# An AdaLN block with attention and a two-of-eight expert layer: merged attention loads, filler products in every free step, earlier first loads, later gates, and a shorter router pipeline

## The chip, the cores and the metric

The kernel runs on one NeuronCore of a Trainium2 chip. It is one program with one launch. TensorE (PE) multiplies, VectorE (DVE) and ScalarE (ACT) work element by element, GpSimd (POOL) does the rest, and SyncE (SP) issues most transfers between the chip's memory (DRAM, for short) and the on-chip memory. The metric is the device time of one execution in microseconds, and lower is better. Of three runs of the kernel before, the median is 2024.34 us (2022.81 to 2042.44).

## The reference, cut to what matters

x is (2, 2048, 256), float32 throughout. H = 16 heads of 16, 6 lattice and 6 hex codes, 8 experts with 1024 hidden units.

```
mod = (silu(c) @ wmod).reshape(2, 6, 1, 256)            # sa, ca, ga, sb, cb, gb
ga, gb = (2*(g >= 0) - 1) * max(|g|, 0.25)               # the two gates
h = layernorm(x) * (1 + ca) + sa
q, k, v = split(h @ qkv_w.T)                             # 16 heads of 16
scores = alpha * tanh(q k^T / beta)
       + sigmoid(lam)/2 * tanh(h hex^T) tanh(h hex^T)^T  # one for all heads
       + lattice(head, tanh(h q6^T), tanh(h q6^T))       # per head
x = x + ga * (softmax(causal(scores)) v) @ out_w.T
h = layernorm(x) * (1 + cb) + sb
logits = silu(h @ rw1 + rb1) @ rw2 + rb2                 # 4096 tokens, 8 experts
top 2, softmax of the two
out = x + gb * sum over the two experts of p_e * (silu(h @ w1[e] + b1[e]) @ w2[e] + b2[e])
```

## The kernel before, in words

The program runs stages one after another. `stage_modulation` loads x (4 MB in four parts) and wmod, gets the statistics of every row of x on VectorE, and the six modulation rows of both batches on TensorE; VectorE evacuates them into `modrow` and finishes the gates there (four operations behind a copy for each of the four gate rows, each waited for). `stage_front` holds the projections and the attention. `stage_output` multiplies by out_w, applies ga and adds x. `stage_router` computes logits, chooses two experts for each token and scatters the token's row to its places in `x_rows`. `stage_experts` takes 72 tiles of 128 rows through their expert. Each stage is a block that all engines enter together.

**The attention.** Eight blocks of 512 queries (two batches of four), each with four groups of four heads: 32 iterations. An iteration has a step for every 128 keys that the block sees, three of them on the diagonal, in all 288 steps. A step is: raw scores of four heads (`raw_scores`, TensorE), tanh of 2048 columns (ScalarE), the bilinear part of each head (`bilinear`, TensorE), a sum for each head (`score_sum`, VectorE), exp (ScalarE), a mask on the diagonal (POOL) and the weighted values (`weighted_values`, TensorE). TensorE is three steps ahead with raw scores, there are four buffers of probabilities.

float32 products are made of halves. A raw score contracts 64 rows: q's high and low halves against k's halves (hi, lo, lo, hi). In memory `q_split` and `k_split` keep two halves a head; a load puts them into the 64 rows in several pieces. A bias row set has 50 rows: 24 of the lattice (`lat_split`), 24 of the hex codes (`soft_split`, one for all heads, spread by the load) and two of a guard (`guard_split`).

**Projections.** The parts of a block's projections are T0, T1 (transposes of h), C (codes), Q0 to Q3 (q and k), L (lattice), V0, V1 and G (guard). Blocks 0 and 1 are projected before attention starts (`HEAD_PARTS`), in five banks; the parts of the others are spread over attention steps by `SLOT`, half a part a step. A step without one may have a filler, `keep_clock`: a product whose result nobody reads. `FILL_AT` gives it to a step that is two or more (three or more behind C) behind the last projection. POOL splits codes, lattice, guard and later Q parts into halves (`split_codes`, `split_lattice`, `split_guard`, `split_heads`), and masks, all in one queue. Before it overwrites a half it waits for the stores of the last block's.

**SP's queue in `stage_front`.** It is in order: x of blocks 0 and 1 and the projection weights; the stores of block 0; `load_keys(0)`; V; codes; guard; `load_bias(0)`, `load_values(0)`; x of block 2; the loads of iteration 1; the stores of block 1; and then, step by step, stores as parts are done, loads of iteration it when iteration it-2 is nearly done (`KEYS_AT`, `BIAS_AT`, `VALUES_AT`), and the stores of the output. `load_keys` waits for the stores of all four Q parts of its block and issues ten loads, `load_bias` waits for three kinds of stores and issues six.

**The router.** It is a pipeline over eight blocks of 512 tokens, written by `skewed` with a lag of five: in step m, VectorE places block m-5 and chooses for block m-4, evacuates the logits of block m-3, splits h of block m-1 and normalises block m. TensorE transposes the logits of m-4, ranks m-5, multiplies logits of m-3, transposes m-1 and multiplies the hidden units of m-2 (eight chunks in three banks). ScalarE takes the tanh of the logit difference of m-5 and then eight silus of m-2. POOL scatters eight tiles of a block once it is placed.

Of the kernel before, what the change touches and what calls it, by code (L numbers as in the profile page):

```python
# [146 lines left out]
def build(nc, a, out):  # L147
# [16 lines left out]
    with ExitStack() as ctx:  # L164
# [5 lines left out]
        with ExitStack() as c2:  # L170
# [3 lines left out]
            stage_modulation(nc, a, modrow, ident, scal, shift, rstd, lattice)  # L174
            stage_front(nc, a, dram, modrow, ident, scal, shift, rstd, lattice, rows_sb, x_back)
# [39 lines left out]
def stage_modulation(nc, a, modrow, ident, scal, shift, rstd, lattice):  # L215
    with ExitStack() as ctx:
# [9 lines left out]
        gate = sb("gate", [P, D])  # L226
        gate_abs = sb("gate_abs", [P, D])
        gate_sign = sb("gate_sign", [P, D])
# [21 lines left out]
        def _(sp):  # L250
# [8 lines left out]
            for q in range(1, XQ):  # L259
                load_x(sp, q)  # L260

        @block.scalar
        def _(act):
# [9 lines left out]
            act.activation(rstd[:, :], rstd[:, :], ACT.Sqrt).then_inc(std_ready, 1)  # L273

# [13 lines left out]
        def _(dve):  # L288
# [59 lines left out]
            for b in range(B):  # L348
                for part in range(6):
                    cols = slice((b * 6 + part) * D, (b * 6 + part + 1) * D)  # L350
                    if part % 3 == 0:
                        dve.tensor_copy(modrow[:, cols], mod_ps[:, cols])
                    elif part % 3 == 1:
                        dve.tensor_scalar(modrow[:, cols], mod_ps[:, cols], 1.0, None, ALU.add)
                    else:
                        then_wait(dve.tensor_copy(gate[:, :], mod_ps[:, cols]))
                        then_wait(dve.scalar_tensor_tensor(gate_abs[:, :], gate[:, :], -1.0, gate[:, :],
                                                           ALU.mult, ALU.max))
                        then_wait(dve.tensor_scalar(gate_abs[:, :], gate_abs[:, :], 0.25, None, ALU.max))
                        then_wait(dve.tensor_scalar(gate_sign[:, :], mod_ps[:, cols], 0.0, 2.0,  # L360
                                                    ALU.is_ge, ALU.mult))
# [4 lines left out]
def stage_front(nc, a, dram, modrow, ident, scal, shift, rstd, lattice, rows_sb, x_back):  # L366
    with ExitStack() as ctx:
# [14 lines left out]
        def borrow(n):  # L382
            used[0] += n
            return rows_sb[:, used[0] - n:used[0]]
# [1359 lines left out]
```

## Time and profile before

| | |
|---|---|
| median of three runs | 2024.34 us |
| the profiled execution | 2022.98 us |
| its span | 2021.2 us |
| busy: PE, PEld, DVE, ACT, POOL | 1811.4, 1076.5, 1209.0, 1233.8, 512.2 us |
| mean granted TensorE clock | 0.926 |
| DMA | 280.29 MB in 186101 packets, mean 139 GB/s |
| first product of attention (raw scores, L800) | 102.1 us |
| last filler product (L788) | 1230.1 us |
| filler products | 222 instructions in 111 steps |
| hidden products of the router (L1314) | 1322.4 to 1436.9 us |

The span in 40 equal slices of 50.5 us:

```profile
PE   2868999999999979999999997689559999999997
ACT  1157889989989968999999993234213333333332
POOL 0535331331232333411000001405612222222222
PEclk7768879989989979999999998889779999999999
```

Each digit is a busy share in tenths; PEclk is the TensorE clock that was granted, in tenths of 2.4 GHz. The attention fills the slices from the third to the twenty-fifth, the experts those from the thirtieth on. A filler is two instructions, since a float32 product takes two passes.

### The profile page before, as it was taken

The numbers are of one execution on the slowest core, as the hardware profiler recorded it, in microseconds if no ns is written. First come the engines' busy times: TensorE is split into PE (matmuls) and PEld (weight loads), VectorE is DVE, ScalarE is ACT, GpSimd is POOL, SyncE is SP. The second block draws the span as 40 slices with busy tenths as digits, with TensorE's granted clock in tenths as the row PEclk, the third lists the DMA queues.
The fourth block names the chain that finished last, engine by engine and source line by source line (L and its number), as shares of the span: only waits on it lengthen the run. The fifth ranks groups of instructions, "written<-read, shape, count | busy, mean of one in ns | idle before, by whom it ended". The sixth has DMA issues, their size and how long they took to land. (4 is left out here: it accounts for less than half of the span.)

```text
span 2021.2 us, 33603 instructions
## 1 busy us (share of the span) xinstructions
PE 1811.4 (90%) x10688; PEld 1076.5 (53%) x10689; DVE 1209.0 (60%) x2539; ACT 1233.8 (61%) x1292; POOL 512.2 (25%) x535
## 2 busy tenths in 40 slices
PE   2868999999999979999999997689559999999997
PEld 1333333333334333333333334568459999999997
DVE  7446768878778757778777775867313333333332
ACT  1157889989989968999999993234213333333332
POOL 0535331331232333411000001405612222222222
PEclk7768879989989979999999998889779999999999
DMA  4489674564562477754844404631366666666663
GB/s 152 122 215 187 157 149 102 118 121 110 121 126 70 114 186 147 138 124 108 191 76 76 87 6 133 203 122 69 110 204 182 182 180 175 186 181 181 176 183 79
DMA packets 186101, 280.29 MB, mean 139 GB/s; under 512 B 18512, under 2 KB 120784, under 8 KB 183824
## 3 DMA queue, kind: packets, MB, share of 16 engines
q1 hardware_dynamic: 172272, 259.94, 51.1%
q0 software_dynamic: 13440, 17.97, 4.5%
q8 instruction: 58, 0.95, 0.2%
q10 hardware_dynamic: 288, 1.08, 0.2%
q14 instruction: 43, 0.35, 0.1%
HBM read 213.90 MB, written 65.03 MB: 138 GB/s over the span
## 5 line engine op out<-in xcount | busy, mean ns | idle before, releaser
L963 DVE SCALAR_TENSOR_TENSOR probs<-probs,scal,bil_ps 128x512 f32<-128x512 f32 (+1 forms) x1152 | 788.2, 715 | 286.2 <-PE bil_ps L817 233.5
L896 ACT ACTIVATE probs<-probs 128x2048 f32<-128x2048 f32 (+1 forms) x288 | 522.7, 1815 | 101.5 <-DVE probs L963 101.0
L889 ACT ACTIVATE probs<-raw_ps 128x2048 f32<-128x2048 f32 (+1 forms) x288 | 508.9, 1767 | 28.9 <-PE raw_ps L800 28.4
L817 PE MATMUL bil_ps<-u_mv,w_st 50*128 50x512 f32 (+3 forms) x1280 | 470.9, 469 | 38.0 <-DVE probs L963 33.5
L817 PEld LDWEIGHTS bil_ps<-u_mv,w_st 50*128 50x128 f32 x1280 | 196.3, 192 | 528.9 <-DVE probs L963 448.6
L1635 ACT ACTIVATE hid_t<-fc_ps,b 128x128 f32<-128x128 f32 x576 | 156.3, 382 | 403.4 <-PE fc_ps L1602 236.0
L836 PE MATMUL o_ps<-probs,v_sb 128*32 128x512 f32 (+3 forms) x2560 | 314.5, 575 | 19.4 <-POOL probs L714 13.2
L800 PE MATMUL raw_ps<-q_mv,k_st 64*128 64x512 f32 (+3 forms) x1280 | 270.8, 406 | 15.2 <-DMA q_mv<-q_split 9.5
L1602 PE MATMUL fc_ps<-rows_t,w 128*128 128x128 f32 x2304 | 270.5, 276 | 0.0
L1602 PEld LDWEIGHTS fc_ps<-rows_t,w 128*128 128x128 f32 x2304 | 264.6, 193 | 0.1
L1613 PE MATMUL fc_ps<-w,hid_t 128*128 x1152 | 260.5, 379 | 0.0
L714 POOL TENSOR_SCALAR_AFFINE_SELECT probs<-probs 128x512 f32<-128x512 f32 x128 | 79.5, 634 | 615.6 <-ACT probs L896 614.2
L1613 PEld LDWEIGHTS fc_ps<-w,hid_t 128*128 128x128 f32 x1152 | 213.4, 190 | 26.3 <-issue 0.2
L1576 POOL DMA_INDIRECT out<-y,token x72 | 112.1, 1557 | 432.7 <-DVE y L1687 423.0
L1683 DVE TENSOR_TENSOR y<-fc_ps,b 128x256 f32<-128x256 f32 x72 | 30.6, 424 | 300.3 <-PE fc_ps L1613 300.3
L800 PEld LDWEIGHTS raw_ps<-q_mv,k_st 64*128 64x128 f32 x1280 | 145.1, 196 | 28.3 <-ACT probs L889 9.8
L788 PE MATMUL part_ps<-modrow,ident 128*128 128x512 f32 x222 | 127.5, 657 | 0.0
L836 PEld LDWEIGHTS o_ps<-probs,v_sb 128*32 128x32 f32 x2560 | 54.2, 111 | 96.6 <-issue 78.2
L1361 POOL DMA_INDIRECT x_rows<-rows_sb,place x64 | 62.6, 978 | 103.3 <-DVE place L1390 85.9
L1343 ACT ACTIVATE act_t<-hid_ps,rb 128x512 f32<-128x512 f32 x64 | 44.0, 689 | 61.2 <-PE hid_ps L1314 61.2
L1679 DVE SCALAR_TENSOR_TENSOR gate<-modrow,late 128x256 f32<-128x256 f32 x72 | 35.0, 485 | 46.8 <-DVE share L1672 46.1
L760 PE MATMUL part_ps<-rows_sb 128*128 128x512 f32 x100 | 61.4, 700 | 0.0
(213 smaller groups left out, 1356.9 us busy)
## 6 DMA issues: line engine op xcount, KB each, us to landing
w<-in_w SPq DMA_DIRECT2D x80, 1024.0 KB, 6.0
q_mv<-q_split SPq DMA_DIRECT2D x128, 128.0 KB, 7.6
k_st<-k_split SPq DMA_DIRECT2D x48, 256.0 KB, 8.5
rows<-x_rows SPq DMA_DIRECT2D x72, 130.0 KB, 2.2
v_rows<-rows_sb SPq DMA_DIRECT2D x8, 1024.0 KB, 7.7
o_t<-o_sb SPq DMA_DIRECT2D x32, 256.0 KB, 9.4
k_st<-k_split SPq DMA_DIRECT2D x16, 512.0 KB, 8.6
v_sb<-v_rows SPq DMA_DIRECT2D x8, 1024.0 KB, 13.6
```

What stands on the lines that cost most here:

```text
L714: ins = pool.affine_select(out=tri, in_=tri, compare_op=ALU.is_ge, fill=0.0, base=0, pattern=[[0, HG], [1, P]], channel_multiplier=-1)
L788: pe.matmul(part_ps[:, :], ident[:, :], modrow[:, 0:BLK], start=True, stop=True)
L800: mm = pe.matmul(raw_ps[:, hd, column:column + width], k_st[row:row + ROWS, p, hd // 2, kt * P:(kt + 1) * P], q_mv[row:row + ROWS, p, hd / ...
L817: mm = pe.matmul(bil_ps[:, hd % 2, column:column + width], w_st[row:row + BIAS_ROWS, b, kt * P:(kt + 1) * P], u_mv[row:row + BIAS_ROWS, p, ...
L836: mm = pe.matmul(o_ps[hd * VW:(hd + 1) * VW, query:query + width], v_sb[:, p, kt, hd * VW:(hd + 1) * VW], probs[:, s % NBUF, hd, column:co ...
L889: act.activation(probs[:, s % NBUF, :, first:BLK], raw_ps[:, :, first:BLK], ACT.Tanh).then_inc(tanh_ready, 1)
L896: act.activation(scores, scores, ACT.Exp).then_inc(exp_ready, 1)
L963: dve.scalar_tensor_tensor(scores, scores, scal[:, ALPHA:ALPHA + 1], bil_ps[:, hd % 2, first:BLK], ALU.mult, ALU.add).then_inc(sum_ready, 1)
L1576: pool.indirect_dma_start(out, bass.IndirectOffsetOnAxis(ap=token[:, u:u + 1], axis=0), y[:, u % 2, :], None, compute_op=ALU.add).then_inc ...
L1602: mm = pe.matmul(fc1_ps[:, p, hc * P:(hc + 1) * P], w1[:, q, k, hc * P:(hc + 1) * P], rows_t[:, p, k * P:(k + 1) * P], start=(k == 0), sto ...
L1613: mm = pe.matmul(fc2_ps[:, p, 0:D], hid_t[:, p, hc * P:(hc + 1) * P], w2[:, ds(e * (HC * D) + hc * D, D)], start=(hc == 0), stop=(hc == HC ...
L1635: silu = act.activation(hid_t[:, p, cols], fc1_ps[:, p, cols], ACT.Silu, bias=b1[:, ds(e * HC + hc, 1)])
```

## The change

It does seven things.

1. `q_split` and `k_split` keep four halves a head, in the order in which the rows are contracted, so each Q part is stored in four pieces. Keys are loaded by one transfer and queries by one.
2. Lattice, codes and guard are stored into one tensor, `u_split`, of 50 rows a head; the six soft rows are stored once for each of 16 heads, by a source that repeats. A bias load is two transfers.
3. Block 0's Q2 and Q3 are stored by ScalarE's queue, its other parts in the order Q0, Q1, C, L by SP's.
4. Every step without a projection gets a filler. Behind C it is one of 64 output rows, beside the codes' 12, and doesn't wait.
5. The first loads of x and the projection weights are issued in the modulation stage, behind its own.
6. The gates are only copied in the modulation, two of four groups of columns by ScalarE. The output stage finishes all four gate rows at once, before its first tile.
7. The router's lag is three: block m-3 is chosen, ranked and placed in the step in which its logits are multiplied; TensorE ranks it between the fourth and the fifth hidden chunk.

```
@@ schedule
-        if half != 0 and s >= last + (3 if o == "C" else 2):
-            FILL_AT[s] = (i, o)
+        assert half != 0
+        FILL_AT[s] = (i, o)
@@ scratch tensors
-    scratch("q_split", (B * H * 2 * HD, T))
-    scratch("k_split", (B * H * 2 * HD, T))
-    scratch("lat_split", (B * H * 4 * HEX, T))
-    scratch("soft_split", (B * 4 * HEX, T))
+    scratch("q_split", (B * H * 4 * HD, T))
+    scratch("k_split", (B * H * 4 * HD, T))
+    scratch("u_split", (B * H * BIAS_ROWS, T))
-    scratch("guard_split", (B * H * 2, T))
@@ stage_modulation, SP, behind its own loads
+            for i in range(EARLY):
+                row = BLOCKS[i][0] * T + BLOCKS[i][1] * BLK
+                sp.dma_start(x_blk[:, i, :, :], a["x"][row:row + BLK, :].rearrange("(t p) d -> p t d", p=P)
+                             ).then_inc(xb_in[i], 16)
+                if i == 0:
+                    sp.dma_start(wcode[:, :, :], a["code_wt"].rearrange("(k p) n -> p k n", p=P)).then_inc(p_in, 16)
+                    sp.dma_start(wqkv[:, :, :], a["qkv_wt"].rearrange("(k p) n -> p k n", p=P)).then_inc(p_in, 16)
...
@@ stage_modulation, ScalarE
+            act.wait_ge(mod_done, 1)
+            for b in range(B):
+                cols = slice((b * 6 + 2) * D, (b * 6 + 4) * D)
+                act.activation(modrow[:, cols], mod_ps[:, cols], ACT.Copy)
@@ stage_modulation, VectorE
-                    if part % 3 == 0:
+                    if part % 3 == 1:
+                        dve.tensor_scalar(modrow[:, cols], mod_ps[:, cols], 1.0, None, ALU.add)
+                    elif part in (0, 5):
                         dve.tensor_copy(modrow[:, cols], mod_ps[:, cols])
-                    else:
-                        then_wait(dve.tensor_copy(gate[:, :], mod_ps[:, cols]))
...
@@ stage_front
+        def store_heads(eng, i, m):
+            b, c = BLOCKS[i]
+            halves = (qk_hi, qk_lo, qk_hi, qk_lo) if m < 2 else (qk_hi, qk_lo, qk_lo, qk_hi)
+            for part, src in enumerate(halves):
+                eng.dma_start(part_rows("q_split" if m < 2 else "k_split", H, 4, HD,
+                                        slice((m % 2) * 8, (m % 2) * 8 + 8), part, b, c),
+                              src[:, m, :].bitcast(F32)).then_inc(st_qk[m], 16)
@@ store of C
-                        sp.dma_start(part_rows("soft_split", 1, 4, HEX, slice(0, 1), part, b, c),
-                                     (s_hi, s_lo)[part % 2][HEX:HROWS, :].bitcast(F32)).then_inc(st_s, 16)
+                        src = (s_hi, s_lo)[part % 2][HEX:HROWS, :].bitcast(F32).rearrange("r (o t) -> r o t", o=1)
+                        sp.dma_start(bias_rows(i, (4 + part) * HEX, HEX).rearrange("z h r t -> r (z h) t"),
+                                     src.broadcast_to([HEX, H, BLK])).then_inc(st_s, 16)
@@ load_keys
-                for z in range(2):
-                    row = z * ROWS
-                    load(k_st[row:row + 2 * HD, p, :, seen], k_both[z])
...
+                for dst, name, cols in ((k_st[:, p, :, seen], "k_split", seen), (q_mv[:, p, :, :], "q_split", own)):
+                    rows = heads(name, ROWS, i, g, cols).rearrange("(j r) t -> r j t", r=2 * ROWS)
+                    sp.dma_start(dst.bitcast(F32), rows).then_inc(keys_in[p], 16)
@@ load_bias
-                    load(u_mv[row:row + n, p, :, :], lat[z])
-                    load(u_mv[row + n:row + 2 * n, p, :, :], sf.broadcast_to([n, HG // 2, BLK]))
-                    load(u_mv[row + 2 * n:row + BIAS_ROWS, p, :, :], gd[z])
+                    sp.dma_start(u_mv[z * ROWS:z * ROWS + BIAS_ROWS, p, :, :].bitcast(F32), rows[z]
+                                 ).then_inc(bias_in[p], 16)
@@ SP, head of the stage
-            for o in ("Q0", "C", "Q1", "Q2", "L", "Q3"):
+            for o in ("Q0", "Q1", "C", "L"):
                 store(0, o)
@@ keep_clock
                 if o == "C":
-                    pe.wait_ge(code_ready, i + 1)
+                    pe.matmul(part_ps[ROWS:P, :], ident[:, ROWS:P], modrow[:, 0:BLK], start=True, stop=True)
@@ ScalarE, block 0
+                if i == 0:
+                    for m in (2, 3):
+                        act.wait_ge(emptied, EMPTIED[i, f"Q{m}"])
+                        store_heads(act, i, m)
@@ stage_output, VectorE
+            gates = modrow[:, :].rearrange("p (g s d) -> p g s d", s=3, d=D)[:, :, 2, :]
+            dve.scalar_tensor_tensor(gate_abs[:, :, :], gates, -1.0, gates, ALU.mult, ALU.max).then_inc(gate_step, 1)
+            dve.tensor_scalar(gate_sign[:, :, :], gates, 0.0, 2.0, ALU.is_ge, ALU.mult)
+            dve.wait_ge(gate_step, 1)
+            dve.tensor_scalar(gate_abs[:, :, :], gate_abs[:, :, :], 0.25, None, ALU.max).then_inc(gate_step, 1)
+            dve.wait_ge(gate_step, 2)
+            dve.scalar_tensor_tensor(gates, gate_sign[:, :, :], -1.0, gate_abs[:, :, :], ALU.add, ALU.mult
+                                     ).then_inc(gate_step, 1)
@@ stage_router, TensorE: order within a step
-                if active(4): transpose of the logits      (first in the step)
-                if active(5): rank
                 if active(3): logit products
                 if active(1): transposes of h
+                if active(3): transpose of the logits
-                if active(2): hidden, chunks 0 to 7
+                if active(2): hidden(m - 2, u % 2, range(HC // 2))
+                if active(3): rank
+                if active(2): hidden(m - 2, u % 2, range(HC // 2, HC))
@@ stage_router, ScalarE, ahead of the silus
-                if active(5):
-                    act.wait_ge(logit_diff_ready, m - 5 + 1)
+                if active(3):
+                    act.wait_ge(logit_diff_ready, m - 3 + 1)
@@ stage_router, VectorE: order within a step
-                if active(5): place_rows(m - 5)
-                if active(4): choose(m - 4)
                 if active(3): copy of the logits
                 if active(1): the two splits of h
+                if active(3): choose(m - 3); place_rows(m - 3)
                 if active(0): normalise(m, u)
```

The router's lines are shortened here to their order; what each does has not changed.

## Rows read from the trace of the kernel before

**Rows 1.** Stages: span, busy us of PE, PEld, DVE, ACT, POOL; PEclk, DMA share, GB/s.

```profile
102.00:190.00 88.00, 67.18 (x338) 28.59 (x339) 46.62 (x75) 52.41 (x33) 40.07 (x48) 0.71 0.92 208
...
700.00:760.00 60.00, 47.20 (x258) 19.91 (x258) 35.88 (x57) 40.02 (x25) 25.69 (x28) 0.80 0.75 178
...
1000.00:1210.00 210.00, 209.43 (x1103) 79.17 (x1103) 162.40 (x236) 202.71 (x117) 9.96 (x16) 1.00 0.36 65
```

**Rows 2.** Eight stretches of low clock, columns as in group 1: first and sum.

```profile
230.00:245.00 15.00, 13.47 (x58) 4.98 (x56) 11.00 (x17) 11.01 (x7) 3.37 (x3) 0.66 0.90 254
...
sum 105.00, PE 97.21 PEld 33.70 DVE 61.70 ACT 76.51 POOL 45.13; mean PE 12.15 PEld 4.21 DVE 7.71 ACT 9.56 POOL 5.64
```

**Rows 3.** Timeline of two full steps, start us, us, engine: tanh, filler, tanh.

```profile
1204.05 1.87 ACT L889 ACTIVATE probs<-raw_ps 128x2048 f32<-128x2048 f32 x1
...
1205.03 1.13 PE L788 MATMUL part_ps<-modrow,ident 128*128 128x512 f32 x2
...
1211.30 1.86 ACT L889 ACTIVATE probs<-raw_ps 128x2048 f32<-128x2048 f32 x1
```

**Rows 4.** Timeline of the modulation, first and last evacuation, and of the first normalisation.

```profile
27.68 0.42 DVE L352 COPY modrow<-mod_ps 128x256 f32<-128x256 f32 x1
...
38.52 0.42 DVE L362 SCALAR_TENSOR_TENSOR modrow<-gate_sign,gate_abs 128x256 f32<-128x256 f32 x1
...
43.35 0.41 DVE L472 TENSOR_SCALAR rows_sb<-rows_sb,rstd,shift 128x256 f32<-128x256 f32 x1 [4.40 <-DMA rows_sb<-in_x]
```

**Rows 5.** Timeline of VectorE at the start of the output stage.

```profile
1234.22 0.28 DVE L1151 MEMSET blank<- 128x260 f32 x1 [3.41 <-PEq L367]
...
1239.81 0.26 DVE L1163 RECIPROCAL rden<-o_tr_ps 128x16 f32<-128x16 f32 x1 [2.77 <-PE o_tr_ps L1099]
```

**Rows 6.** DMA, 10 to 24 us, in 40 slices: busy tenths and GB/s, x and wmod.

```profile
DMA  9999999999999999999999999999994000000000
GB/s 404 456 386 404 345 342 360 357 351 345 360 342 345 354 348 348 345 354 348 351 337 351 351 351 348 339 360 342 360 275 135 23 0 0 0 0 0 0 0 0
```

**Rows 7.** DMA, 130 to 140 us, keys, queries and bias, in 40 slices.

```profile
DMA  9998999999999999999899998778999899987998
...
DMA packets 1235, 1.85 MB, mean 185 GB/s; under 512 B 253, under 2 KB 428, under 8 KB 1233
```

**Rows 8.** DMA, 64 to 68 us, the two stores of Q0, in 40 slices.

```profile
DMA  0000576292420913344743564448353554455445
GB/s 0 0 0 0 143 123 61 20 82 20 41 20 0 102 20 82 123 164 164 246 164 143 205 266 184 164 164 287 123 184 143 225 225 184 164 225 225 184 164 205
```

**Rows 9.** Timeline of POOL and of PE, the first iterations.

```profile
89.70 0.60 POOL L664 CAST w_hi<-code 12x512 fp32r<-12x512 f32 x1
...
114.67 1.81 POOL L714 TENSOR_SCALAR_AFFINE_SELECT probs<-probs 128x512 f32<-128x512 f32 x3
...
139.81 1.22 PE L800 MATMUL raw_ps<-q_mv,k_st 64*128 64x512 f32 x4 [9.48 <-DMA q_mv<-q_split]
```

**Rows 10.** Timeline of one router step.

```profile
1382.93 0.71 PE L1314 MATMUL hid_ps<-h_hi,rw_hi 128*128 128x512 f32 x2
...
1384.67 0.69 ACT L1343 ACTIVATE act_t<-hid_ps,rb 128x512 f32<-128x512 f32 x1 [3.48 <-PE hid_ps L1314]
...
1384.94 1.21 DVE L1452 CAST h_hi<-tr_ps 128x1024 fp32r<-128x1024 f32 x1
```

**Rows 11.** Timeline of the end of the router.

```profile
1438.06 1.96 PE L1293 MATMUL log_ps<-act_t,rw 128*32 128x128 f32 x64 [0.30 <-ACT act_t L1343]
...
1444.75 0.18 DVE L1394 TENSOR_TENSOR logits<-lgt_ps,rb 128x32 f32<-128x32 f32 x1
...
1446.28 0.17 DVE L1406 TENSOR_TENSOR logit_diff<-top 128x4 f32<-128x4 f32 x1
...
1450.35 0.16 DVE L1390 CAST place<-place_f 128x8 uint32<-128x8 f32 x1
...
1469.28 0.96 POOL L1361 DMA_INDIRECT x_rows<-rows_sb,place  x1 [0.31 <-issue]
```

More of the change, by code:

```diff
@@ L415, in stage_front @@
         part_ps = ps("part_ps", [P, BLK])
-        p_in, pad_ready, ones_ready = sem("p_in"), sem("pad_ready"), sem("ones_ready")
-        x_in = [sem(f"xb_in{p}") for p in range(2)]
+        pad_ready, ones_ready = sem("pad_ready"), sem("ones_ready")
         h_ready, part_mm, emptied, code_ready, hi_ready = (
@@ L489, in load_rows, with bias_rows @@
                              ).then_inc(x_in[i % 2], 16)
+            def bias_rows(i, first, n):
+                view = dram["u_split"].rearrange("(z h r) t -> z h r t", h=H, r=BIAS_ROWS)
+                b, c = BLOCKS[i]
+                return view[b:b + 1, :, first:first + n, c * BLK:(c + 1) * BLK]
             def store(i, o):
@@ L507, in store @@
                         sp.wait_ge(lo_ready, 4 * (i - EARLY) + m + 1)
-                    for part, src in enumerate((qk_hi, qk_lo)):
-                        sp.dma_start(part_rows("q_split" if m < 2 else "k_split", H, 2, HD,
-                                               slice((m % 2) * 8, (m % 2) * 8 + 8), part, b, c),
-                                     src[:, m, :].bitcast(F32)).then_inc(st_qk[m], 16)
+                    store_heads(sp, i, m)
                 elif o == "L":
@@ L1305, in step, with hidden @@
                     tr.then_inc(tr_mm, 1)
+                if active(3):
+                    pe.wait_ge(log_ready, m - 3 + (LOG_0 + 1))
+                    pe.transpose(lgt_ps[:, 0:P], log_sb[:, :], ident[:, :]).then_inc(lgt_mm, 1)
                 if active(2):
[L1307 to L1316 removed]
+                    hidden(m - 2, u % 2, range(HC // 2))
+                if active(3):
+                    n = m - 3
+                    pe.wait_ge(rank_step, n * N_RANK + N_RANK)
+                    flat = lambda t: t.rearrange("p t e -> p (t e)")
+                    pe.matmul(rank_ps[:, 0:TPB * E], before[:, :], flat(both[:, :, :]), start=True, stop=False)
+                    pe.matmul(rank_ps[:, 0:TPB * E], all_ones[:, :], flat(seen[:, 0:TPB, :]),
+                              start=False, stop=True).then_inc(rank_mm, 1)
+                if active(2):
+                    hidden(m - 2, u % 2, range(HC // 2, HC))
+            def hidden(n, p, chunks):
+                if chunks[0] == 0:
+                    pe.wait_ge(h2_t_step, n * 2 + (H2T_0 + 2))
+                for hc in chunks:
+                    pe.wait_ge(act_ready, n * HC + (bank_before(hc) + 1 + ACT_0))
+                    terms = [(w, x, k) for w, x in ((rw1_hi, h2_hi), (rw1_hi, h2_lo), (rw1_lo, h2_hi))
+                             for k in range(KC)]
+                    for j, (w, x, k) in enumerate(terms):
+                        mm = pe.matmul(hid_ps[:, hc % HB, :], w[:, k * HID + hc * P:k * HID + (hc + 1) * P],
+                                       x[:, p, k, :], start=(j == 0), stop=(j == len(terms) - 1))
+                    mm.then_inc(hid_mm, 1)
             pe.sem_inc(log_mm, LOGM_0)
@@ L1320, in _ @@
             pe.sem_inc(hid_mm, HIDM_0)
-            skewed(pe, N_RBLK, 5, 2, step)
+            skewed(pe, N_RBLK, 3, 2, step)
             pe.wait_ge(place_ready, N_RBLK + PL_0)
@@ L1465, in _ @@
             dve.wait_ge(seen_ready, 1)
-            skewed(dve, N_RBLK, 5, 2, step)
+            skewed(dve, N_RBLK, 3, 2, step)
             done = [0]
```

124 lines of the change are left out of this document (45 added, 79 removed).

## The prediction

> **What bounds the kernel now.** I read the busy strips of the page first, then a table by stage, then the waits, the DMA view and timelines of the places that the diff touches. Four stretches matter. From 102 to 190 us, the first attention steps, ScalarE is busy 52.4 of 88 us, the DMA engines 92%, and the clock is 0.71 [rows 1]. From 1000 to 1210 us attention runs at its pace: ScalarE 202.7 of 210 us (0.965), TensorE as full, clock 1.00. So a steady step is ScalarE's tanh and exp, 3.62 us ((1211.30 - 1204.05)/2), and a filler product fits into it [rows 3]. Between 190 and 1000 us ScalarE loses time where the clock falls: in eight stretches, 105 us together, it is busy 76.5 us [rows 2], where 0.965 would give 101.3; 24.8 us are lost. In the one at 230 us the step behind a finished G part has neither a projection nor a filler, TensorE idles there, and some ten microseconds at the lower level (1.2 GHz) follow. Last, the experts' stage is TensorE's own chain, and nothing in the change touches it.
>
> **The change, part by part.** The sum is against the profiled execution: 2022.98 us (span 2021.2), 1.4 below the median of 2024.34.
>
> **1. Modulation.** VectorE evacuates and finishes the gates from 27.68 to 38.94 us, and normalises block 0 from 43.35 us, behind loads of x that are issued at its stage's start [rows 4]. Of 24 operations 8 stay, at about 0.34 us each ((38.52 - 27.68)/32 for the mean of 32, short waits in it; so 2.7 us). ScalarE's two copies of 512 columns run beside them. The stage ends near 30.4 us, plus 0.5 for the handover: 30.9. The loads moved forward are 1.8 MB behind the 5.8 MB of x and wmod; those moved at about 350 GB/s with the engines at 9 tenths and were over at about 21 us [rows 6], so the rest takes 5.2 us more, and lands before 30.9. Issuing costs SP's time alone, and SP has nothing else there. Saved: 43.35 - 30.9 = 12.4 us. The row's wait of 4.40 us, less the handover, is for the load of x: if the loads came late, those 3.9 would be paid again, and the term would end at -8.5.
>
> The gates' four operations on 1024 columns come back in the output stage. VectorE is free from 1234.50 and next needed at 1239.81 [rows 5]; an operation on 1024 columns takes 1.21 us [rows 10], so at most 4.9 with short waits. Hidden by the wait for the first transposed tile, 0; without that cover 4.9.
>
> **2. Merged loads, doubled stores, 102 to 190 us.** Keys, queries and bias now go to 16 or 32 partitions at a time. With them in the queue the engines are 9 tenths busy and move 185 GB/s [rows 7]; x into 128 partitions moves 350 at the same share [rows 6]. The merged loads cover 128 partitions (bias 50). A first-block iteration loads 1.4 MB: 7.6 us become 4.0; a second-block one 1.9 MB: 10.3 become 5.4. The schedule asks for iterations 2 to 6 in the stretch, of which about half are second-block ones: some 18 us of DMA time less. SP issues 5 loads an iteration instead of 17, which costs nothing and frees it.
> Against it: each Q part is stored in four pieces instead of two. The stores of Q0 ran at some 180 GB/s with only 4 to 5 tenths busy [rows 8], as if half the engines carried them. Eight more of 256 KB a block at 185 GB/s: 11 us a block on that half. New too is soft, stored 16 times over: 4 x 192 KB a block, all read from six partitions. Nothing in the trace reads like it. Bounds: at the rate of rows 8, 1.0 us each, 4 a block; at the narrow loads' rate scaled by partitions (185 x 6/32 = 35 GB/s) 5.5 each, 22 a block. I take the 22, since a few partitions are what it is nearest to.
> The Trainium skill, "SBUF — State Buffer", section "Door 1: The DMA port swizzle", says that what counts is how many of 16 ports the partitions reach, 27.2 GB/s each; by it the six partitions reach two, and the four on one take about 4.8 us a store, 19 a block. The trace agrees on the loads (185 GB/s on 32 partitions or fewer); no row here shows the store.
> Who waits: POOL splits block 1's codes at 89.70 without a gap, and its mask at 114.67 [rows 9] starts the first weighted values. The change makes that split wait for block 0's soft stores: issued by about 74, beside 11 us of Q, with 22 of their own, they land near 98 or 99, 9 us later (an estimate: Q0's pieces start at 63, twelve pieces of 0.7 us of issue lie ahead, and a wait for Q1). The eight pieces of Q2 and Q3 of block 0 are issued by ScalarE, some 5 us of its queue; nothing of its own is due there until block 1's codes, and its high half of Q3 for block 1 comes after the same 98 us, so 0. Then block 1's stores sit in the queue ahead of the keys of iteration 2, for which TensorE already waits 9.48 us until 139.81 [rows 9]. So the first 40 us get up to 9 longer, and what follows gets back about as much. I take 0; ends -18 (the loads' gain whole, the stores beside it) and +20 (stores 11 + 22 on top of each other for block 1, less 13 won back in the iterations behind).
> The second batch starts at 700 us the same way: 40.0 busy of 60 [rows 1], 17.9 below pace. Part is masks behind POOL's code split, which stays; I take -5, ends -10 and +3.
>
> **3. Fillers.** 62 more steps get one, all those that had neither (173 of 288 steps are without a projection, 111 had a filler). In each stretch of rows 2 such a step stands just ahead. A filler is two products of 0.43 us apart, 1.13 us with its drain [rows 3], beside ScalarE: 0 at full clock. I take three quarters of the 24.8: -18; ends -25 and 0.
>
> **4. Router.** The last logit products end at 1440.02. Now choice and places of block 7 come right behind: 0.9 us for the copy and its transposition, then logits to places 5.76 us (1450.51 - 1444.75), so places at 1446.7 and the first of eight scatters 0.7 later; at 1.27 us each (0.96 + 0.31) the last starts at 1456.3 instead of 1469.28 [rows 11]: -13.
> But ScalarE now waits in every step for the new logit difference before its first silu. VectorE splits h in two operations of 1.21 [rows 10] behind the transposes, to 3.7 us after the logit products; the difference is there 1.7 later (1446.45 - 1444.75) [rows 11], tanh 0.3, first silu done at 6.4. TensorE has three banks; a chunk is 1.4 us (1.74 with the handover [rows 10]), so its fourth could start at 5.0: late by 1.4, in 7 steps, +9. VectorE's own step, 3.7 plus 5.8 for choice and places plus twelve normalising operations of 0.43, is 14.7 us and stays below TensorE's 14.4 + 1.4; what is queued behind the choice, the normalisation of the next block but two, is needed only after the next logit products. Sum -4; ends -13 and +3.
>
> Sum: 2023.0 - 12.4 - 0 - 5 - 18 - 4 = 1983.6.
>
> **Rivals.**
> **Stores saturate** (part 2 at its +20 end): for it, the first stretch is DMA-bound already; against it, the loads halve. 1983.6 + 20 = 2004.
> **Fillers don't lift the clock**: it falls for diagonal steps with thin products. Against it: 1000 to 1210 us has a filler in nearly every step and stays at 1.00 [rows 1]. 1983.6 + 18 = 2002.
> **TensorE becomes the bound, slower**: 62 fillers of 0.86 us on TensorE's own chain, from the point at which its step passes ScalarE's 3.62. TensorE is already busy 209.4 of 210 us [rows 1], which speaks for it; that ScalarE keeps 0.965 there speaks against. 1983.6 + 18 + 53 = 2055.
> **Loads hide everything**: part 2 at -18, router at -13, fillers whole: 1983.6 - 18 - 5 = 1960.
> **It doesn't do what it says**: early loads delay wmod or the modulation's end stays with x, and the router's wait eats its tail: 1983.6 + 4 + 7 + 5 = 2000.
>
> **How the numbers follow.** Chances: forecast 0.50, stores 0.14, no clock 0.12, slower 0.06, more hidden 0.12, not done 0.06. The range leaves out the slower case and half the tails: 1956 to 2014. About 1% (20 us) is what a measurement tells from no change; faster is below 2004: nearly all of the forecast (0.47), the hidden case, half of stores and of no clock, and half of not done: 0.75. Same 0.18, slower 0.07.
>
> **What would show it.** The first normalisation near 31 us; the first raw scores near 90; block 1's code split on POOL late, with soft's stores as its cause; a merged key load landing at over 300 GB/s; the clock strip without dips behind C and G; ScalarE idle at the head of each router step, TensorE's step 15.8 instead of 14.4 us (eight chunks, logit products of 1.96, transposes); the last scatter 13 us nearer to the logits. Wrong would be: dips that stay, or stores that push iteration 2 beyond the others' gain.

## The result, and the profile after

The change makes the kernel slower: 2106.52 us (median of four runs, 2102.75 to 2113.73) beside 2025.5 for the kernel before on the same chip, a ratio of 1.0386 (95% interval 1.0321 to 1.0451). The profiled execution took 2109.69 us, its span is 2107.9. I had forecast 1983.6.

First the stages, columns as in [rows 1], which they answer.

```profile
102.00:190.00 88.00, 36.07 (x175) 16.53 (x175) 24.95 (x40) 25.93 (x17) 26.50 (x32) 0.58 0.60 175
700.00:760.00 60.00, 54.64 (x334) 23.70 (x333) 41.14 (x66) 46.12 (x31) 27.52 (x32) 0.91 0.41 109
1000.00:1210.00 210.00, 209.43 (x1114) 80.03 (x1111) 162.59 (x236) 202.11 (x116) 10.59 (x17) 1.00 0.31 104
```

In the head ScalarE now works 25.9 us instead of 52.4, while the DMA engines are *less* busy, 0.60 instead of 0.92. The steady stretch is unchanged. A better ruler than equal windows is the start of the same tanh in both profiles (the 288 tanh instructions of attention, one a step), worked out from timelines of ScalarE:

```
tanh of step       1      7     19     25    151    157    163    288
before         102.8  141.1  196.1  217.9  702.3  731.5  762.0 1222.3
changed        +6.6  +36.2  +45.9  +46.3  +31.8  +38.4  +41.0  +40.7
e4  fillers     -6.0   +0.4   +3.0   +3.3  -11.0  -11.4   -9.5  -10.2
e13 soft once   -8.9   +5.0   +1.2   +1.6  -12.8  -13.1  -15.0  -18.5
e10 (below)    -14.4  -16.9  -20.2  -19.8  -34.2  -34.5  -34.7  -36.6
```

So attention loses 30 us between its first and seventh step and 10 more by the 19th, wins 14.5 back to the 151st, and loses 9 again where the second batch starts. The rest comes in the router: from its first transposition of h (1311.25 us before, 1351.85 after) to the experts' first (1483.77 and 1569.1) it takes 217.3 us instead of 172.5.

**The head.** VectorE, POOL and PE in the timeline of the changed kernel: first normalisation, block 1's code split, the gates, and the raw scores of the seventh step, the first of iteration 2.

```profile
30.16 0.41 DVE L491 TENSOR_SCALAR rows_sb<-rows_sb,rstd,shift 128x256 f32<-128x256 f32 x1 [0.31 <-PEq L237]
...
98.05 0.60 POOL L668 CAST w_hi<-code 12x512 fp32r<-12x512 f32 x1 [22.68 <-DMA u_split<-s_lo]
...
175.98 1.22 PE L804 MATMUL raw_ps<-q_mv,k_st 64*128 64x512 f32 x4 [39.36 <-DMA q_mv<-q_split]
...
1274.67 1.16 DVE L1164 SCALAR_TENSOR_TENSOR gate_abs<-modrow 128x1024 f32<-128x1024 f32 x1
...
1277.07 1.22 DVE L1169 SCALAR_TENSOR_TENSOR modrow<-gate_sign,gate_abs 128x1024 f32<-128x1024 f32 x1
...
1281.00 0.26 DVE L1183 RECIPROCAL rden<-o_tr_ps 128x16 f32<-128x16 f32 x1 [2.52 <-PE o_tr_ps L1110]
```

The normalisation starts 13.2 us earlier than in [rows 4], and the gates fit ahead of a wait of 2.52 us that was 2.77 [rows 5]. But 39.36 us of wait stand where 9.48 stood [rows 9]. Why, the queue of SP shows (start, time to issue):

```profile
118.44 0.45 SPq L526 DMA_DIRECT2D u_split<-s_hi  x1
...
121.21 0.27 SPq L526 DMA_DIRECT2D u_split<-s_lo  x1
121.54 3.93 SPq L481 DMA_DIRECT2D q_split<-qk_hi  x1
125.52 4.52 SPq L481 DMA_DIRECT2D q_split<-qk_lo  x1
130.08 5.21 SPq L481 DMA_DIRECT2D q_split<-qk_hi  x1
135.34 4.80 SPq L481 DMA_DIRECT2D q_split<-qk_lo  x1
140.18 4.59 SPq L481 DMA_DIRECT2D k_split<-qk_hi  x1
...
165.63 1.55 SPq L565 DMA_DIRECT2D k_st<-k_split  x1
```

Behind block 1's four soft stores the next five stores of 256 KB take 3.9 to 5.2 us each to get into the queue, where one took about 0.6 when the queue was free. The keys of iteration 2 are issued at 165.63 us. Meanwhile the stages show what runs:

```profile
125.00:130.00 5.00, 5.00 (x27) 1.30 (x21) 1.65 (x3) 1.06 (x1) 0.69 (x2) 0.74 0.40 77
...
140.00:145.00 5.00, 0.00 (x0) 0.00 (x0) 0.00 (x0) 0.00 (x0) 0.00 (x0) 0.50 0.33 52
...
165.00:170.00 5.00, 0.00 (x0) 0.00 (x0) 0.00 (x0) 0.00 (x0) 0.00 (x0) 0.50 1.00 317
```

A share of 0.33 to 0.40 of sixteen DMA engines is the time of five or six engines, which move 52 to 77 GB/s. Then, while the merged key load runs, the share is 1.00 at 317 GB/s. The engines that are busy are slower too: 52 GB/s on 0.33 of sixteen is 9.8 GB/s each, and 317 GB/s on all of them is 19.8 each. The Trainium skill, "DMA: Bandwidth & Descriptors", section "Why a DMA increments its semaphore by 16 and not by 1", says that a transfer issued from SP uses the largest number of engines, up to sixteen, that divides the outermost size of both sides; for the soft store, outermost six rows, that is six. The trace agrees with the share (six of sixteen is 0.375). The profile doesn't tell the engines apart, though, and the rule leaves the halved pace of each open: six engines at 19.8 GB/s would move 119 (an estimate from the last row).

**The router.** TensorE and POOL in one step of the changed kernel; [rows 11] has the same logit products in one piece of 1.96 us.

```profile
1460.61 0.69 ACT L1368 ACTIVATE act_t<-hid_ps,rb 128x512 f32<-128x512 f32 x1 [0.67 <-PE hid_ps L1339]
...
1461.35 1.50 PE L1303 MATMUL log_ps<-act_t,rw 128*32 128x128 f32 x42 [0.78 <-issue]
...
1462.49 0.96 POOL L1386 DMA_INDIRECT x_rows<-rows_sb,place  x1 [0.30 <-issue]
...
1463.07 0.39 PE L1303 MATMUL log_ps<-act_t,rw 128*32 128x128 f32 x3 [0.23 <-issue]
...
1464.49 0.43 PE L1303 MATMUL log_ps<-act_t,rw 128*32 128x128 f32 x4 [0.43 <-issue]
...
1465.92 1.09 PE L1303 MATMUL log_ps<-act_t,rw 128*32 128x128 f32 x5 [1.01 <-issue]
...
1469.38 1.97 PE L1313 MATMUL tr_ps<-ident,h_blk 128*128 128x128 f32 x8
...
1475.62 0.21 ACT L1362 ACTIVATE prob_diff<-logit_diff 128x4 f32<-128x4 f32 x1 [12.07 <-DVE logit_diff L1431]
```

The 64 products take 8 us, with holes "until issue": nothing that the profile shows is waited for. The transpositions behind these run at half clock (1.97 us for eight instead of 1.09). The products have such holes in the seven steps that have scatters of POOL beside them, where they take 3.8 to 8.1 us; in the first, which has none, they take 1.95. With or behind the holes of the first six the granted clock falls to 0.5 for 3.4 to 6.8 us, and hidden products run at half pace there (1.06 us for two instead of 0.62 at 1449 us); so the clock has a part in what the holes cost. A step takes 22.4 us (places at 1387.8 and 1544.3, seven steps) instead of 14.67. ScalarE's long wait of 12 us, which I had feared, is mostly TensorE's lateness: in e3 below, where the products have no holes, it is 4.5 to 6.4 us.

### The profile page after: what moved, and what is told of

Read it like the earlier page. It is cut to its first block and busy times, and to the rows that moved or that the text cites. A ratio compares the mean times of both kernels' runs of the same rounds, so it can differ in the third digit from the quotient of the medians.

```text
span 2107.9 us, 33735 instructions
## 1 busy us (share of the span) xinstructions
PE 1860.9 (88%) x10812; PEld 1095.3 (52%) x10813; DVE 1208.2 (57%) x2523; ACT 1234.5 (59%) x1294; POOL 513.8 (24%) x535
## 5 line engine op out<-in xcount | busy, mean ns | idle before, releaser
L821 PE MATMUL bil_ps<-u_mv,w_st 50*128 50x512 f32 (+3 forms) x1280 | 463.1, 458 | 11.4 <-DVE probs L971 6.1
L840 PE MATMUL o_ps<-probs,v_sb 128*32 128x512 f32 (+3 forms) x2560 | 304.5, 558 | 28.4 <-POOL probs L718 16.8
L792 PE MATMUL part_ps<-modrow,ident 128*128 128x512 f32 x326 | 189.0, 662 | 0.0
L792 PEld LDWEIGHTS part_ps<-modrow,ident 128*128 128x128 f32 x326 | 49.7, 192 | 38.8 <-issue 37.4
```

Of the source, the lines that this page charges most:

```text
L792: pe.matmul(part_ps[:, :], ident[:, :], modrow[:, 0:BLK], start=True, stop=True)
L821: mm = pe.matmul(bil_ps[:, hd % 2, column:column + width], w_st[row:row + BIAS_ROWS, b, kt * P:(kt + 1) * P], u_mv[row:row + BIAS_ROWS, p, ...
L840: mm = pe.matmul(o_ps[hd * VW:(hd + 1) * VW, query:query + width], v_sb[:, p, kt, hd * VW:(hd + 1) * VW], probs[:, s % NBUF, hd, column:co ...
```

## The experiments

Ratios are against the kernel before on the same chip, with 95% intervals; one point of a hundred is 20 us.

**Undoing the parts one by one.** e1 stores soft once:

```
-  src = (s_hi, s_lo)[part % 2][HEX:HROWS, :]....rearrange("r (o t) -> r o t", o=1)
-  sp.dma_start(bias_rows(i, (4 + part) * HEX, HEX)..., src.broadcast_to([HEX, H, BLK]))
+  sp.dma_start(part_rows("soft_split", 1, 4, HEX, slice(0, 1), part, b, c), (s_hi, s_lo)[part % 2][HEX:HROWS, :]...)
   ...
+  load(u_mv[row + n:row + 2 * n, p, :, :], sf.broadcast_to([n, HG // 2, BLK]))
```

> The changed kernel, but soft is stored once per block (four stores of six rows) and repeated for the heads by the load, as before; Q, K, keys, modulation, fillers and router as changed. Theory S (the sixteen-fold soft store chokes SP's queue): in the changed kernel the first tanh is at 109.5 us, the seventh at 177.3, and the 157th step is 9.5 us later against the kernel before than the 151st. Without the store the first tanh is near 90 us, the seventh near 128, nothing is lost at 740 us, and the time is about 2106.5 - 68 = 2038 us. Rival Q (the doubled stores of Q and K are the choke): the seventh tanh stays beyond 160 us and the time is above 2090.

Measured: 2003.75 us, ratio 0.9911 (0.9887 to 0.9936). The seventh tanh is at 144.9, and the second batch gains 5.7 us (step 151 to 181). Theory S holds for the choke, though the seventh tanh had been expected near 128; rival Q falls. It took 34 us less than expected, because the router's holes were gone too (170.9 us for 217.3), though its router is the changed one. That became the question of the later runs.

e2 takes `stage_router` from the kernel before.

> The changed kernel with the router stage of the kernel before (choice and places four and five blocks behind). The first transposed router block to the last scatter takes 159 us before and 203 us after. Theory: the whole of that is in the router's step, so the time is 2106.5 - 44 = 2062 us, and TensorE's 64 logit products take 1.95 us in each step again. Rival (what comes into the stage is different too: rows, clock): the gain is below 35 us.

Measured: 1.0209 (1.0167 to 1.0251), 2063.47 us, router 172.2 us. As expected.

e3 moves the scatters:

```
   pool.wait_ge(place_ready, n + 1 + PL_0)
+  if n + 1 < N_RBLK:
+      pool.wait_ge(log_mm, n + (LOGM_0 + 2))
```

> The changed kernel, with one more wait on POOL: the eight scatters of a block start only when the logit products of the next block are done. Theory F (TensorE runs out of instructions while POOL scatters): the 64 logit products, 4 to 9 us in seven of the eight steps now, take 1.95 us, a step takes some 16 to 18 us instead of 22.4, and the time is 2106.5 - 30 = 2076 us, or a little less. Rival C (the chain logits, choice, ScalarE's wait is what makes the step long) and rival L (the loop is entered twice instead of once): the logit products keep their holes, and the time is within 5 us of 2106.

Measured: 1.0242 (1.021 to 1.0273), 2069.48 us. All eight groups of logit products take 1.95 us, a step 16.5. C, the rival I had priced in the prediction, falls: the chain of choice and ScalarE's wait is still there and costs 1.8 us a step. Theory F isn't shown by this run alone, since e1, on the same chip, had no holes without the wait either. e9 and e18 show it, below.

e4 is the kernel before with the fillers: `FILL_AT[s] = (i, o)` for every step without a part, and C's filler into rows 64 to 127 without the wait for the codes.

> The kernel before with the 62 further filler steps alone. Theory: the clock strip stays at 9 from 300 to 700 us, and the time is about 2024 - 16 = 2008 us (the changed kernel gains 15.9 us on the kernel before between the 25th and the 151st step). Rival (it is the merged loads that gain there): within 4 us of 2024. Rival (62 fillers load TensorE's own chain): above 2030.

Measured: 0.9952 (0.9929 to 0.9975), 2013.79 beside 2020.81 us: 9.7 us by the ratio, and 14.3 between the 25th and the 151st step of its profile, where the clock is 0.99 instead of 0.93. e4 has no merged loads, so they aren't needed for that gain.

**Are the holes the kernel's?** e5 is the changed kernel again. e6 adds an unused `scratch("soft_split", (B * 4 * HEX, T))`. e11 has e3's wait with `LOGM_0 + 1`, which has long passed. e12 puts 40 increments of an unused semaphore ahead of TensorE's steps.

> The changed kernel once more, nothing altered. In its first profile TensorE's 64 logit products had holes in seven of eight router steps; with soft stored once (same TensorE and POOL code in the router, the scatters lying over the same logit products) they had none. Theory G (the holes belong to one chip or one placement of a run, not to the kernel): none here, the router takes 157 us from the first transposition to the last scatter, and the time is 2106.5 - 44 = 2062 us. Theory F (scatters over logit products, whenever they meet): holes again, 2106 us. Theory P (where the DRAM tensors of this kernel lie): holes again, 2106 us.

> The changed kernel with an unused DRAM tensor of 48 x 2048 ahead of the code tensor, so that what follows it in DRAM lies where it lies in the kernel with soft stored once. Theory P (placement in DRAM makes the holes): none here, 2106.5 - 44 = 2062 us, while the unaltered kernel has them. Theory F: holes, 2106 us. Theory G: as the unaltered kernel beside it.

> The changed kernel with one more wait on POOL in each block ahead of its scatters, for a value that the logit products have passed long before: POOL's code is as long as in the kernel with later scatters, but nothing moves. Theory F: the holes stay, 2106 us. Rival A (where POOL's code lies decides): they vanish, 2062 us.

> The changed kernel with 40 increments of an unused semaphore on TensorE ahead of the router's steps, so that the code of its loop lies 40 instructions further on. Theory F: the holes stay where they are in each step, 2106 us. Rival A' (where TensorE's code lies decides): holes at other products, or none, and a time between 2062 and 2106.

Measured: 1.0365 (1.0316 to 1.0413); 1.0408 (1.0359 to 1.0458); 2108.98 and 2112.57 us, one run each. All four have the holes, in the same seven steps. P, A and A' fall, and so does G in the form that the changed kernel has holes only on its first chip; that a chip or a session can be free of them comes back with e13.

**Stores and loads of Q and K.** e7 is e1 with Q and K stored in two pieces and loaded in ten, as before; e10 is e7 with the router of before; e8 is e1 with that router; e9 is e7 with e3's wait.

```
-  halves = (qk_hi, qk_lo, qk_hi, qk_lo) if m < 2 else (qk_hi, qk_lo, qk_lo, qk_hi)
+  for part, src in enumerate((qk_hi, qk_lo)):
```

> The changed kernel with soft stored once and, further, each Q and K part stored in two pieces and loaded in ten, as before; modulation, fillers and router stay as changed. With soft stored once the first tanh was 9.5 us earlier than in the kernel before, the seventh 3.9 us later, and 5.7 us came back between the 151st and the 181st step. Theory (eight more pieces a block cost in the head what the merged loads give back later): the seventh tanh is near 132 us instead of 144.9, the second batch gives back nothing, and the time is 2003.8 - 13 + 6 = 1997 us. Rival (the merged loads win in the head too): above 2006.

> The changed kernel with soft stored once and with the router of the kernel before. The new router without holes took 170.9 us from its first transposition to the experts' first, the old one 172.6. Theory (the new router is worth nearly nothing, either way): 2003.8 + 1.7 = 2005.5 us. Rival (holes come and go with the new router in the executions that were only timed): a lower time than 2000.

> The changed kernel with soft stored once and Q and K stored in two pieces and loaded in ten, as before (its attention was 37.3 us ahead of the kernel before at the last step, its router had the holes: 217 us from the first transposition to the experts' first against 172.6), and POOL's scatters of a block behind the logit products of the next. Theory F (holes only where scatters lie over logit products): no holes, the router takes 175 us, and the time is 2038.2 - 217 + 175 = 1996 us. Rival A (the holes hang on where the code lies, not on the scatters): they may stay, 2038 us.

> The same without the later scatters, and with the router of the kernel before. Theory: attention is 37.3 us ahead and the router as before, so 2028 - 37 = 1991 us, the fastest of all so far. Rival (the attention's lead of 37.3 us was one profile's): above 2003.

Measured: e7 1.0041 (1.0015 to 1.0068), a miss of 41 us, all of it holes again (router 216.5 us); its attention did more than was expected, seventh tanh at 124.3 for 132. e8 0.9925 (0.99 to 0.9949), as expected within the interval. e9 0.9899 (0.9868 to 0.993), 2007.31 us for the 1996 expected: the wait takes the holes away on the chip on which e11 and e12 have them, which is the first evidence for F. PE and POOL in the timeline of e9, in one step:

```profile
1384.78 1.95 PE L1315 MATMUL log_ps<-act_t,rw 128*32 128x128 f32 x64 [0.78 <-ACT act_t L1380]
1387.57 1.09 POOL L1400 DMA_INDIRECT x_rows<-rows_sb,place  x1 [7.85 <-PE log_ps L1315]
```

e10 **0.9894** (0.9859 to 0.9929), 2004.86 us beside 2026.77, is with e9 the lowest ratio of all, though e1's 0.9911 can't be told from them. The 1991 us expected were a miss, and the rival's "above 2003" came true. Only the profiled execution came near (1996.85; all four took 1996.85 to 2011.08), so much of the 37.3 us of lead was one profile's. The head varies between runs of one code: e9's seventh tanh is at 129.8 and its 19th at 186.6, e10's are at 124.2 and 175.9.

**The converse, and e1 again.** e14 is the kernel *before*, its scatters delayed onto logit products that they do not touch there:

```
+  if n + 3 < N_RBLK:
+      pool.wait_ge(hid_mm, (n + 3) * HC + (HIDM_0 + 6))
```

> The kernel before with one more wait on POOL: the scatters of blocks 0 to 4 start when the sixth hidden chunk of the block three later is done, so that they run over the logit products that follow, which no scatter touches in the kernel before. Theory F: holes in the logit products of blocks 3 to 7, each 2 to 6 us long in all, TensorE being the bound here: 2024 + 5 x 5 = some 2050 us. Rival A (holes belong to the new router's code or order, not to the overlap): none, 2024 us within 5.

> The changed kernel with soft stored once, the same as e1, beside the changed kernel itself (e16) on one chip. In e1 the scatters lay over the logit products and there were no holes; in every other kernel with that overlap there were. Theory G' (that chip, or that placement, had no holes to give): where e16 shows holes, this shows them too, and the time is 2003.8 + 44 = 2048 us. Rival (something in this kernel keeps them away): no holes, 2004 us.

> The changed kernel, unaltered, as control for e13 and e14 on the same chip. Theory F: holes as in its three profiles so far, 2106 us. Theory G': holes here and in e13, or in neither.

Measured: e14 1.0185 (1.0132 to 1.0239), 2066.71 us. Blocks 0 to 2 have their logit products in 1.96 us, blocks 3 to 7 have holes and need 9.3 to 16.3 us. PE and POOL in the timeline of e14, in the step of block 4:

```profile
1395.55 0.96 POOL L1363 DMA_INDIRECT x_rows<-rows_sb,place  x1 [14.41 <-PE hid_ps L1314]
...
1398.24 1.89 PE L1293 MATMUL log_ps<-act_t,rw 128*32 128x128 f32 x46 [0.30 <-ACT act_t L1343]
...
1401.12 0.38 PE L1293 MATMUL log_ps<-act_t,rw 128*32 128x128 f32 x2 [0.99 <-issue]
...
1404.40 0.96 POOL L1363 DMA_INDIRECT x_rows<-rows_sb,place  x1 [0.30 <-issue]
1405.42 0.41 PE L1293 MATMUL log_ps<-act_t,rw 128*32 128x128 f32 x1 [1.07 <-issue]
```

Old router, old order, one more wait on POOL: on this chip the overlap alone makes the holes. e13 gives 1.0109 (1.0055 to 1.0162), 2051.14 us, with holes, and e16 beside it 2115.08 (one run) with holes. So e1 was an exception of its session, perhaps of its chip (it ran beside e2, e3 and e4, none of which has the overlap), not of its code. PE and POOL in e1, and then in e13:

```profile
1368.15 1.17 POOL L1391 DMA_INDIRECT x_rows<-rows_sb,place  x1 [0.30 <-issue]
...
1369.14 1.95 PE L1308 MATMUL log_ps<-act_t,rw 128*32 128x128 f32 x64 [0.86 <-ACT act_t L1373]
...
1369.62 1.17 POOL L1391 DMA_INDIRECT x_rows<-rows_sb,place  x1 [0.30 <-issue]
```

```profile
1404.56 0.96 POOL L1391 DMA_INDIRECT x_rows<-rows_sb,place  x1 [0.30 <-issue]
1404.68 1.50 PE L1308 MATMUL log_ps<-act_t,rw 128*32 128x128 f32 x42 [0.78 <-issue]
...
1406.45 0.38 PE L1308 MATMUL log_ps<-act_t,rw 128*32 128x128 f32 x3 [0.27 <-issue]
...
1407.86 0.41 PE L1308 MATMUL log_ps<-act_t,rw 128*32 128x128 f32 x4 [1.04 <-issue]
```

The same code under the same overlap, with and without holes: 0.0198 of the time, 40 us (28 to 52 with both intervals). In e1 the scatters lie over the products as well, but TensorE does not starve.

**The modulation alone.** e15 is e10 with the old fillers.

> The kernel before with the modulation's part of the change alone: first loads issued in the modulation, gates evacuated by ScalarE and finished later, the order of the first stores, and ScalarE issuing the stores of Q2 and Q3 of block 0. Router, fillers, stores of two pieces and loads of ten are as before. Predicted gain 12.4 us; e10, which has the fillers too, stands at 0.9894 of the kernel before and the fillers alone at 0.9952, so theory: 0.994, some 2013 us beside 2025. Rival (the gain is the fillers', or noise of the head): within 4 us of the kernel before.

Measured: 0.9937 (0.9914 to 0.9959), 2016.55 us: 12.8 us by the ratio.

**What of the soft store costs.** e17 writes the sixteen copies from DRAM, e18 adds e3's wait:

```
+  once = dram["soft_split"][b * n:(b + 1) * n, c * BLK:(c + 1) * BLK]
+  sp.dma_start(bias_rows(i, n, n)..., once.rearrange("(o r) t -> o r t", o=1).broadcast_to([H, n, BLK]))
```

> The changed kernel, but soft is stored once per block (four stores of six rows) and its sixteen copies are written by one DRAM to DRAM transfer of 768 KB, issued ahead of the block's lattice stores; loads of the bias stay merged. Theory N (the store chokes the queue because only six engines carry it): the seventh tanh is near 146 us as with soft stored once, not 177, and the time is that of e13, about 2051 us with the router's holes. Rival B (the bytes, and the wait for them ahead of the load): the seventh tanh stays beyond 165 us, and the time is above 2085.

> The same, with POOL's scatters behind the next block's logit products. Theory N with F: no holes, 2051 - 37 = 2014 us, a little below the kernel before (2025). Rival B: 2050.

Measured: e17 1.0114 (1.0057 to 1.0171) beside e13's 1.0109, seventh tanh at 147.9; e18 0.9974 (0.9947 to 1.0001), all logit products without holes, on the chip on which e17 has them. So the sixteenfold bytes cost little (the two ratios agree within 16 us); what cost is how they were carried. e17 changes two things at once, though: the copies have sixteen outermost rows instead of six, and they are read from DRAM instead of six partitions. Whether the few engines or the few partitions (the prediction's ports) set the pace was not separated. The stages of e17 where the changed kernel crawled:

```profile
120.00:125.00 5.00, 4.98 (x37) 2.66 (x39) 3.40 (x6) 3.26 (x2) 0.00 (x0) 0.69 0.74 189
125.00:130.00 5.00, 2.18 (x16) 1.08 (x8) 3.87 (x7) 3.35 (x3) 4.17 (x5) 1.00 0.98 193
130.00:135.00 5.00, 0.00 (x0) 0.00 (x0) 0.00 (x0) 0.00 (x0) 1.00 (x2) 0.50 0.90 302
```

## Why the prediction was wrong, point by point

Prices by ratios, times 2024 us:

```
modulation (e15)                     -12.8  +- 4.6   predicted -12.4
soft stored 16 times (e2 - e8)       +57    +- 10    \
doubled stores, merged loads          +6    +- 9      | predicted 0 and -5
   (e8 - e10; e7 from e13: +14 +- 12)                /
fillers (e4)                          -9.7  +- 4.7   predicted -18
router without holes (e1 - e8)        -3    +- 7     predicted -4
holes (e13 - e1)                     +40    +- 12    not seen
sum                                  +78, measured +78
```

That the sum closes shows less than it seems: e1 cancels in it, and e8 stands in it with either sign. What it tests is that e15 and e4 together give e10 (0.9889 for 0.9894), and that e13 less e8 (+37) gives the changed kernel less e2 (+36). Two lines have a second price. For the soft store, attention ends 39.9 us behind the kernel before in e2's profile and 18.6 ahead in e8's, 58.5 apart. For the holes, e17 less e18, on one chip, gives 28 +- 13, with what the late scatters cost counted in.

**1. Modulation: right.** The first normalisation came at 30.16 us where I had 30.9, and the gates were hidden. The first raw scores, which I wanted near 90 us, came at 108.2 because of point 2; with soft stored once they come at 92.0.

**2. Loads and stores: wrong, and the largest miss.** The failed step is "the first 40 us get up to 9 longer, and what follows gets back about as much. I take 0", and its bound of +20. The price of the store was right: block 1's code split came at 98.05 us for the forecast 98 or 99, and 22 us a block is about what block 1's stores show (from 118 to 144 us). What I priced wrongly is who stands behind. I added the DMA time of the stores and set the loads' gain against it, as if transfers shared the engines. But SP's queue is in order, and the rows read as if it were full: behind the soft stores five of block 1's stores cost SP 3.9 to 5.2 us each, and the keys of iteration 2 come 40 us later (165.63 for 125.15). The gain of the loads can't begin while the loads stand at the end of the queue, though most of the DMA engines' time is idle. I had also counted it once: it comes back with block 2 (7 us between the 16th and 17th step) and at the start of the second batch (9 us), where I forecast a gain of 5. That gain is real without the store: 5.7 us in e1, 4.0 in e13. The merged loads' own merit is nil or less: at 317 GB/s they run as forecast, yet kernels with two stores and ten loads are faster by 6 +- 9 and 14 +- 12 us, which I put down to the doubled stores that merged loads need. No run has one without the other.

**3. Fillers: right in kind, too large.** The dips are gone (clock 0.99 for 0.93 from 218 to 704 us) and the steps from the 25th to the 151st win 14.5 us. I had three quarters of 24.8; it is 0.58 of it there and 9.7 us in the whole, since a part of the gain was lost again at the second batch (e4 has 11.4 us at step 157 and 9.5 at step 163), where attention waits for other things. TensorE did not become the bound.

**4. Router: the term was right, and a mechanism was missing.** Without holes the new router is worth -3 +- 7 us, for the -4 of the sum. ScalarE's wait makes a step 16.5 us instead of 14.67, a little more than "late by 1.4, in 7 steps", and the end is as forecast: the last scatter starts 16.5 us behind the last logit product instead of 29.3. What I left out is where the work that hangs on the moved step lands. I priced when the choice and the last scatter come, but not where the other scatters fall: POOL's eight a block hang on the places and move with them, from beside the hidden products, which TensorE takes at 0.23 us each, onto the logit products, which it takes at 0.03. The sum has nothing for this; the holes cost 40 +- 12 us, or 28 +- 13 by the pair on one chip. No row of the kernel before shows the two together, so the profile could not price it; it could have shown that they never met.

The rival that ended on the slow side, TensorE as bound through fillers, was the wrong one. "Stores saturate" had the right place and a third of the size.

## What to carry to other kernels

A DMA issued in order is not only its bytes: work out how many engines and partitions carry it, and then what is queued behind it and cannot start. When a step of a pipeline moves, list what it releases on other engines, and look which instructions that work will now lie over; here the run of 64 short products was the sensitive one. And when an experiment gains more than its theory says, as e1 did, repeat it before explaining.

## What the runs showed of the hardware that I had not expected

While POOL issues indirect DMAs, TensorE can run dry in a run of short matmuls: 41 to 57 pairs of weight load and product at 0.03 us, then pairs in groups of mostly one to six with holes of 0.1 to 1.1 us. In the kernel before the same products take 1.95 us. This was so in the changed kernel's three profiles, in e6, e7, e11, e12, e13, e14 and e17, and not in e1. Moving the scatters off the products took it away in e9 and e18, on the chip where e11, e12 and e17 have it.

TensorE shows no such holes in its hidden products of 0.23 us, but ScalarE can be late beside them. That is why the router of the kernel before takes 180 us in e8, e10 and e15 and 171 to 173 elsewhere. ScalarE in the timeline of e15, in the step of block 4:

```profile
1393.22 0.69 ACT L1375 ACTIVATE act_t<-hid_ps,rb 128x512 f32<-128x512 f32 x1 [0.67 <-issue]
1395.57 0.69 ACT L1375 ACTIVATE act_t<-hid_ps,rb 128x512 f32<-128x512 f32 x1 [1.67 <-PE hid_ps L1346]
1398.44 1.84 ACT L1375 ACTIVATE act_t<-hid_ps,rb 128x512 f32<-128x512 f32 x3 [2.18 <-PE hid_ps L1346]
```

TensorE's chunks go on at 1.36 us each until then, so the second of these silus was due at 1394.58 and the next at 1395.94: they start 1.0 and 2.5 us late, and TensorE's logit products wait for the last. e8 and e10 have the same two in the same places; the kernel before (its profile's chip is not on record), e2 and e4 have none. A step with both takes 15.6 us instead of 14.67, and the last step 17.3 to 18.7 instead of 13.8. With late scatters it is the same: e9 and e18 have such silus (a router of 182 and 183 us), e3 has none (174.5). So all four kernels of e1's chip are free of it, in ScalarE as in TensorE, and each of the fourteen on the three other chips has it in one engine or the other.

What runs short, and why that one chip or session was spared, is open. In the changed kernel the hole is not the fetch of code from DRAM, as no instruction packet moves between 1457 and 1470 us while the products above are pulled apart. That the first 41 pairs or more run at full rate would fit a queue that is drained faster than it is refilled, but that is argued, not shown. The changed kernel was not run in e1's session.
